# Two layers of graph convolution on one core: half of the attention transposes through VectorE's 32x32 blocks and DRAM

## What is computed

```python
h = max(layernorm(x), 0)                                  # 128 x 512
feats = einsum('nf,hfu->hnu', h, W)                       # 8 heads of 64 units
dense = leaky_relu(e_self[:, :, None] + e_neigh[:, None, :], 0.2)
att = softmax(dense + (-1e10) * (1 - A))                  # 8 x 128 x 128
x = x + relu(concat(att @ feats) + b)
h = max(layernorm(x), 0)
r = relu(hypergraph_conv(h, adj, W1, b1))                 # 128 x 1024
y = hypergraph_conv(layer_norm(r) * gamma + beta, adj, W2, b2)
out = x + (y + h)                                         # 128 x 512
```

## Time and profile before

| | before |
|---|---|
| median of three runs | 2489.99 us (2489.61 to 2491.07) |
| profiled execution, its own time | 2479.36 us |
| span of its instructions | 2477.6 us |
| TensorE (PE) busy | 2419.2 us, 98% |
| VectorE (DVE) busy | 1976.4 us, 80% |
| ScalarE (ACT) busy | 1763.3 us, 71% |
| GpSimd (POOL) busy | 1368.0 us, 55% |
| moved by DMA | 336.69 MB in 656793 packets |

### The profile page before, as it was taken

One profiled execution on the slowest core, in us unless ns is written; L12 is line 12 of the kernel. 1 busy time (PEld: TensorE's weight loads), 2 busy tenths in 40 slices (PEclk: granted clock), 3 DMA queues, 4 the chain that ended last, 5 costly groups with the idle time before them and its releaser, 6 DMA issues.

```text
span 2477.6 us, 50428 instructions
## 1 busy us (share of the span) xinstructions
PE 2419.2 (98%) x14004; PEld 2101.6 (85%) x14004; DVE 1976.4 (80%) x4373; ACT 1763.3 (71%) x4489; POOL 1368.0 (55%) x1549
## 2 busy tenths in 40 slices
PE   5799999999999999999999999999999999999997
PEld 3688888888888888888888888888888888888886
DVE  3888888888888888888888888888888888888884
ACT  2677777777777777777777777777777777777774
POOL 2465555565565565565555555555555556556543
PEclk8899999999999999999999999999999999999999
DMA  5344454455445445445445445445454444445442
GB/s 206 95 139 138 136 140 137 134 140 140 134 139 141 134 139 141 134 138 142 132 138 143 131 139 143 125 145 139 128 142 137 134 138 138 137 137 138 138 113 72
DMA packets 656793, 336.69 MB, mean 136 GB/s; under 512 B 554752, under 2 KB 571136, under 8 KB 656768
## 3 DMA queue, kind: packets, MB, share of 16 engines
q1 hardware_dynamic: 636256, 298.64, 43.5%
q10 hardware_dynamic: 20512, 37.76, 4.3%
HBM read 235.03 MB, written 101.26 MB: 136 GB/s over the span
## 4 chain that ended last, share of the span: by engine, by line
PE 95%; DMA 2%; DVE 1%; issue 1%; ACT 1%; POOL 0%; SPq 0%; POOLq 0%; DVEq 0%; ACTq 0%
PE p_w1a L853 15%; PE p_w1a L858 14%; PE p_w1a L854 14%; PE p_att L927 9%; PE p_w1b L854 5%; PE p_w1b L858 5%; PE p_w1b L853 5%; PE p_w1b L957 5%; PE p_att L907 4%; PE p_fa L849 3%; PE p_fa L847 3%; PE p_fa L848 3%; PE p_fb L847 2%; PE p_fb L848 2%; PE p_fb L849 2%; PE p_tb L847 1%
## 5 line engine op out<-in xcount | busy, mean ns | idle before, releaser
L338 POOL TENSOR_TENSOR u<-u,mask 128x1024 f32<-128x1024 f32 x128 | 306.6, 2395 | 761.4 <-DMA u<-en_rows 761.4
L438 ACT ACTIVATE att<-u,shifts 128x128 f32<-128x128 f32 x1024 | 402.3, 393 | 133.0 <-DVE shifts L740 131.6
L853 PE MATMUL p_w1a<-W_hi,rT_hi 128*128 128x512 f32 x1024 | 416.8, 407 | 1.5 <-ACT rT_hi L561 1.5
L854 PE MATMUL p_w1a<-W_lo,rT_hi 128*128 128x512 f32 x1024 | 405.9, 396 | 0.0
L439 ACT ACTIVATE att_low<-u,shifts 128x128 f32<-128x128 f32 x1024 | 399.6, 390 | 0.0
L731 DVE TENSOR_REDUCE neg_max<-u 128x8 f32<-128x1024 f32 x128 | 156.1, 1220 | 149.9 <-POOL u L338 149.9
L858 PE MATMUL p_w1a<-W_hi,rT_lo 128*128 128x512 f32 x1024 | 259.5, 395 | 0.0
L392 POOL TENSOR_TENSOR z_lo<-raw,z_hi 128x512 fp32r<-128x512 f32 x128 | 165.7, 1294 | 154.9 <-ACT z_hi L547 154.9
L927 PE MATMUL p_att<-feats,attT 128*128 128x65 f32 x2048 | 243.1, 272 | 3.1 <-ACT attT L483 3.1
L927 PEld LDWEIGHTS p_att<-feats,attT 128*128 128x128 f32 x2048 | 239.5, 192 | 3.9 <-ACT attT L483 3.9
L547 ACT ACTIVATE z_hi<-raw 128x512 fp32r<-128x512 f32 x128 | 81.1, 634 | 221.6 <-DVE raw L797 221.6
(11 more groups left out here) (121 smaller groups left out, 6759.7 us busy)
## 6 DMA issues: line engine op xcount, KB each, us to landing
u<-en_rows SPq DMA_DIRECT2D x130, 576.0 KB, 3.6
r_blocks<-raw SPq DMA_DIRECT2D x128, 512.0 KB, 2.6
raw<-r_blocks SPq DMA_DIRECT2D x512, 128.0 KB, 3.2
xT_in<-in_xT SPq DMA_DIRECT2D x128, 256.0 KB, 3.9
out<-raw SPq DMA_DIRECT2D x128, 256.0 KB, 2.0
x_in<-in_x ACTq DMA_DIRECT2D x124, 256.0 KB, 3.6
adj_in<-in_adj SPq DMA_DIRECT2D x128, 128.0 KB, 2.5
en_rows<-eT SPq DMA_DIRECT2D x520, 1.1 KB
```

The costliest lines, as they stand in the source:

```text
L338: nc.gpsimd.tensor_tensor(u[:, g.slot(2), 0:HEADS, :], u[:, g.slot(2), 0:HEADS, :], mask[:, :].unsqueeze(1).broadcast_to([P, HEADS, N]), A ...
L438: nc.scalar.activation(att[:, i, :], u[:, g.slot(2), i, :], ACT.Exp, bias=shifts[:, 0, i:i + 1])
L853: mm(dst, hi, w_hi, start=first, stop=False)
L854: mm(dst, hi, w_lo, start=False, stop=False)
```

## The change

Heads 4 to 7 stay as they were: transposed by TensorE (now four instructions) and copied out of PSUM by ScalarE (now 512 columns wide). Heads 0 to 3 take another way. VectorE transposes `att` of these heads by 32x32 blocks into a new tile attB, behind z in its turn, two graphs ahead (graph t+2 in turn t). One turn later SP writes attB to DRAM ahead of the attention terms, and reads it back behind the broadcast of u in four DMAs, one for each block column, in runs of 32 elements (128 bytes), straight into attT. TensorE now multiplies heads 4 to 7 first, then waits for the reads and multiplies heads 0 to 3.

Two more edits go with it. The attention terms (eT) are written to DRAM by one DMA of all 128 partitions instead of four of nine; en_rows has 32 rows for it. And the columns of W1 and of b1 are permuted on the host, so that the reads of r_blocks can take runs of 256 elements (1 KB) instead of 32; the copies to rT_hi and rT_lo then put the chunks in order through their access patterns (`rT_chunks`).

```diff
         neg_max = sb("neg_max", [P, HEADS])
+        attB = sb("attB", [P, HH * N])
         attT = sb("attT", [P, HEADS, N])
         rden = sb("rden", [P, HEADS])
...
         rT = raw[:, 0, DH:2 * DH]
+        rT_chunks = rT.rearrange("p (q k a) -> p k q a", q=4, a=32)
         rT_hi, rT_lo = sb("rT_hi", [P, DH], F32R), sb("rT_lo", [P, DH], F32R)
...
-        en_rows = nc.dram_tensor("en_rows", [ROWS, N], F32, kind="Internal").ap()
+        en_rows = nc.dram_tensor("en_rows", [32, N], F32, kind="Internal").ap()
...
+        att_blocks = nc.dram_tensor("att_blocks", [P, HH * N], F32, kind="Internal").ap()
...
+                if t.plus(1).within(NG):
+
+                    sp.wait_ge(s_attB, t.plus(1).count())
+                    sp.dma_start(att_blocks[:, :], attB[:, :]).then_inc(s_attB_out, 16)
                 if g.within(NG + 2):
 
                     sp.wait_ge(s_eT, g.count())
-                    for q in range(4):
-                        sp.dma_start(en_rows[:, 32 * q:32 * (q + 1)], eT[32 * q:32 * q + ROWS, :]).then_inc(s_en_out, 16)
-                    sp.wait_ge(s_en_out, g.count(per=64))
+                    sp.dma_start(en_rows.rearrange("h (q a) -> q h a", a=32), eT[:, :]).then_inc(s_en_out, 16)
+                    sp.wait_ge(s_en_out, g.count(per=16))
                     sp.dma_start(u[:, g.slot(2), :, :].rearrange("p h n -> p (h n)"),
-                                 en_rows.rearrange("(a h) n -> a (h n)", a=1).broadcast_to([P, ROWS * N])).then_inc(s_en_bc, 16)
+                                 en_rows[0:ROWS, :].rearrange("(a h) n -> a (h n)", a=1).broadcast_to([P, ROWS * N])).then_inc(s_en_bc, 16)
+                if t.plus(1).within(NG):
+
+                    sp.wait_ge(s_attB_out, t.plus(1).count(per=16))
+                    for c in range(4):
+                        sp.dma_start(attT[32 * c:32 * (c + 1), 0:HH, :].rearrange("b k (q a) -> b k q a", q=4),
+                                     att_blocks.rearrange("(q b) (k c a) -> c b k q a", q=4, c=4, a=32)[c]).then_inc(s_attD, 16)
                 g = t.plus(-2)
                 if g.within(NG):
 
@@ -289,8 +302,8 @@
                     sp.dma_start(r_blocks[:, :], rB).then_inc(s_rB_out, 16)
                     sp.wait_ge(s_rB_out, g.count(per=16))
                     for c in range(4):
-                        sp.dma_start(rT[32 * c:32 * (c + 1), :].rearrange("a (k q b) -> a k q b", q=4, b=32),
-                                     r_blocks.rearrange("(q a) (k c b) -> c a k q b", q=4, c=4, b=32)[c]).then_inc(s_rT, 16)
+                        sp.dma_start(rT[32 * c:32 * (c + 1), :].rearrange("a (q n) -> a q n", q=4),
+                                     r_blocks.rearrange("(q a) (c n) -> c a q n", q=4, c=4)[c]).then_inc(s_rT, 16)
...
                 act.wait_ge(s_shifts, g.count())
                 if g.has(1):
-                    act.wait_ge(s_attT, g.count(1))
+                    act.wait_ge((s_attB, s_attT)[half], g.count(1))
                     act.wait_ge(s_att, g.count(1, per=2))
...
-                    nc.scalar.activation(attT[:, :, :].rearrange("p h n -> p (h n)"), p_att[:, :],
+                    nc.scalar.activation(attT[:, HH:HEADS, :].rearrange("p h n -> p (h n)"), p_att[:, HALF:2 * HALF],
                                          ACT.Copy).then_inc(s_attT_sb, 1)
...
                     act.wait_ge(s_rT, g.count(per=64))
                     if g.has(1):
                         act.wait_ge(s_w2, g.count(1))
-                    nc.scalar.activation(rT_hi[:, :], rT, ACT.Copy).then_inc(s_rT_hi, 1)
+                    nc.scalar.activation(rT_hi[:, :].rearrange("p (k q a) -> p k q a", q=4, a=32), rT_chunks, ACT.Copy).then_inc(s_rT_hi, 1)
...
                     dve.wait_ge(s_rT_hi, g.count())
-                    nc.vector.tensor_tensor(rT_lo[:, :], rT, rT_hi[:, :], ALU.subtract).then_inc(s_rT_lo, 1)
+                    nc.vector.tensor_tensor(rT_lo[:, :].rearrange("p (k q a) -> p k q a", q=4, a=32), rT_chunks,
+                                            rT_hi[:, :].rearrange("p (k q a) -> p k q a", q=4, a=32), ALU.subtract).then_inc(s_rT_lo, 1)
...
                     nc.vector.scalar_tensor_tensor(z[:, :], p_w1a[:, :], rs2[:, g.slot(2):g.slot(2) + 1], t_bc[:, :],
                                                    ALU.mult, ALU.add).then_inc(s_z, 1)
+                g = t.plus(2)
+                if g.within(NG):
+
+                    dve.wait_ge(s_att, g.count(per=2) - 1)
+                    if g.has(1):
+                        dve.wait_ge(s_attB_out, g.count(1, per=16))
+                    nc.vector.transpose(attB[:, :], att[:, 0:HH, :].rearrange("p h n -> p (h n)")).then_inc(s_attB, 1)
...
                     pe.wait_ge(s_att, g.count(per=2))
                     if g.has(1):
                         pe.wait_ge(s_osc, g.count(1))
-                    for i in range(HEADS):
+                    for i in range(HH, HEADS):
                         last = nc.tensor.transpose(p_att[:, i * N:(i + 1) * N], att[:, i, :], ident[:, :])
                     last.then_inc(s_attT, 1)
...
                     pe.wait_ge(s_attT_sb, g.count())
                     pe.wait_ge(s_feats_sb, g.count(per=2))
-                    for i in range(HEADS):
-                        last = mm(p_o[:, i // HH, i % HH, :], attT[:, i, :], feats[:, g.slot(2), i, :], start=True, stop=True)
+                    for i in range(HH, HEADS):
+                        mm(p_o[:, i // HH, i % HH, :], attT[:, i, :], feats[:, g.slot(2), i, :], start=True, stop=True)
+                    pe.wait_ge(s_attD, g.count(per=64))
+                    for i in range(HH):
+                        last = mm(p_o[:, 0, i, :], attT[:, i, :], feats[:, g.slot(2), i, :], start=True, stop=True)
                     last.then_inc(s_o, 1)
...
+    def by_blocks(a):
+
+        return a.reshape(a.shape[:-1] + (-1, 4, 32)).swapaxes(-3, -2).reshape(a.shape)
...
-        "W1T": np.asarray(L1_gnn_W1).T, "b1": L1_gnn_b1,
+        "W1T": by_blocks(np.asarray(L1_gnn_W1).T), "b1": by_blocks(np.asarray(L1_gnn_b1)),
```

2 lines of the change are left out of this document (1 added, 1 removed).

## The result

The changed kernel takes 2475.11 us (median of four runs, 2472.43 to 2477.38) beside 2490.53 us for the kernel before in the same rounds (2489.61 to 2493.04). The ratio is 0.9938 with a 95% interval of 0.9924 to 0.9953: it is faster, by 0.6%. The forecast was 2439 us with a range up to 2466: the direction was right, but 15 of 51 us came.

The account below looks back on a forecast made before the run. TensorE was taken to bound the kernel: 55.4 us off for the transposes, less 2.5 for VectorE's lateness and 1.5 for the ramp, is 51.4, from 2489.99 to 2439 us. The range was 2430 to 2466.

Parts of the forecast that it names:

- Removed from TensorE: Four of eight transposes on TensorE go, 0.44 us per turn; over 126 turns 55.4 us off.
- Edge one: ScalarE's halved copy of transposed heads ends 0.13 us before TensorE's product wants it, as before.
- The block transpose: VectorE's new instruction with 512 elements per partition adds 0.65 us to the chain through u.
- The strided copies to rT_hi and rT_lo: Taking r's chunks in order by access pattern costs VectorE under 0.02 us each.
- From eT to eT: VectorE's chain from turn to turn through u takes 17.89 of 18.53 us, its waits for others being outside it.
- VectorE's idle time ahead of hg_lo shrinks: Sign expected in the profile after: this wait falls from 0.6 to under 0.2 us per turn.
- Edge two: Chain through u: transpose costs 0.65, single write gains 0.6; 17.94 us stays below TensorE's turn of 18.09.
- Edge three: Reads into attT, queued behind u, land 0.4 us before TensorE wants them; called the least certain edge.
- part of the gain is eaten by VectorE: Rival: smaller write gain or dearer VectorE work makes the chain through u bound the turn; 2448 to 2485 us, chance 0.23.

Follow-up runs that it names:

- e8: The kernel before, with ScalarE rounding hg_hi ahead of z_hi; ratio 0.995 to the kernel before.
- e7: The changed kernel with hg_hi rounded ahead of z_hi and VectorE's block transpose cut to 32 of 512 columns; ratio 0.9762 to the kernel before.
- e16: The changed kernel with hg_hi rounded ahead of z_hi and r's reads again in runs of 32 elements; ratio 0.9878 to the kernel before.
- The exchange: Two roundings on ScalarE swapped, hg_hi ahead of z_hi; in the changed kernel ratio 0.9875 to the kernel before, in the kernel before itself 0.995.
- e1: The changed kernel with the attention terms written by four DMAs of nine rows again; ratio 1.0073 to the kernel before.
- e17: The changed kernel with hg_hi rounded ahead of z_hi, without the write of attB and the reads into attT; ratio 0.9774 to the kernel before.
- e18: The changed kernel with hg_hi rounded ahead of z_hi, attB written but no reads into attT; ratio 0.9772 to the kernel before.
- e6: The changed kernel with ScalarE rounding hg_hi ahead of z_hi; ratio 0.9875 to the kernel before.
- e10: The changed kernel with hg_hi rounded ahead of z_hi and the first four heads' features computed behind eT; ratio 0.9869 to the kernel before.
- e15: The changed kernel with hg_hi rounded ahead of z_hi, two reads into attT ahead of u and two behind; ratio 1.0379 to the kernel before.
- e5: The changed kernel with the block transpose moved behind eT, rT_lo behind y and attB written behind the attention terms; ratio 1.0361 to the kernel before.
- e12: The changed kernel with hg_hi rounded ahead of z_hi and `larger` for half 0 ahead of the wait for G_rs; ratio 0.9898 to the kernel before.
- e9: The changed kernel: hg_hi ahead of z_hi, block transpose behind eT, attB written behind the terms, adj tests beside GpSimd's mask; ratio 1.0325 to the kernel before.

## Why the prediction was right in direction and wrong in size

- **Removed from TensorE, 0.44 us per turn**, was right. In the mean of the turns the transposes take 0.355 us from their first start to the next matmul instead of 0.792; the attention product in two parts takes 1.73 instead of 1.70. From e8 to e7, on the same chip, the turn went from 18.61 to 18.26 us, 0.35 us, and e7 still stands still for 0.09.
- **Edge one** held: the copy takes 0.58 us, and TensorE waits for ScalarE's part of attT 2.3 us in four times.
- **The block transpose** was priced at 0.65 us; it takes 0.63 in VectorE's queue. The strided copies to rT_hi and rT_lo cost nothing (1.05 and 1.21 us; with plain copies, e16, the time is the same).
- **The step that failed: "From eT to eT a turn has only these spots in which VectorE waits for something outside the chain: 0.42 us for hg_hi ... The chain itself thus takes 18.53 - 0.64 = 17.89 us."** hg_hi was not outside. It stood on ScalarE behind z_hi, which waited for VectorE's z. The chain was thus just below TensorE's turn and not 0.64 us below it: the row "changed" adds to 18.63 us where the prediction has 17.94. The transpose filled that wait and changed z to hg_lo from 2.03 to 2.05 us, so it cost next to nothing, but the room that was to take up every other lateness was not there. The exchange shows its share: 0.9938 to 0.9875, 16 us. The sign "VectorE's idle time ahead of hg_lo shrinks" came true and said nothing. (The 18.53 us are one turn; the mean is 18.65, which moves the chain and TensorE's turn alike.)
- **Edge two, the single write, gain 0.6 us**: the right mechanism, mis-sized. It measured 0.26 us, which e1 loses again. The issue itself takes 0.59 us, where I had allowed the 0.34 of a small DMA; the rest lies behind it: from the end of the issue to u's it is 1.41 us, 0.89 before. The spread over the engines was as assumed. The DMA queue in the half microsecond in which the terms move (packets, MB, share of 16 engines' time):

```profile
q1 hardware_dynamic: 129, 0.02, 20.5%
```

  That is 0.205 x 16 x 0.5 = 1.64 us of engine time, moved within some 0.4 us: about four engines. The rule of the Trainium skill that the prediction named (DMA: Bandwidth & Descriptors, "Why a DMA increments its semaphore by 16 and not by 1") gives four, and the trace agrees.
- **Edge three, the reads.** They are in time, as said. But I asked only whether u delays them, not whether they delay u. "Queue behind u on the same sixteen engines" made them harmless to u; they cost it 0.15 to 0.3 us per turn, on the chain: 1.0%, 26 us (with the exchange, e17 against e16). The prediction's sum has no term for this.
- Together: without reads and with the exchange the ratio is 0.977 (e17, e18). The forecast, 2439 / 2490, is 0.980. The two causes, 16 and 26 us, are together enough for the 36 us that were missing. How the 36 divide between them is not shown: each was measured on another base, and the exchange also gains 0.5% in the kernel before, which is no part of the forecast's error. With the exchange on both sides the change is worth 0.75% with the reads (e6, e8) and 1.8% without them (e17, e8), where 2.0% was forecast. The rival "part of the gain is eaten by VectorE" came nearest: its condition (the single write gains less) was met and 2475 us lies in its span of 2448 to 2485. Its price of 2457 us was missed, since it began from 17.89 too (and by its own terms is 2490 - 35 + 1.5 = 2456).

The best complete kernel is the changed one with hg_hi ahead of z_hi: 2455.11 us against 2487.22, ratio 0.9875 (e6); e10 is equal to it. A way to bring the blocks back without reads beside u was not found: in the turn they are needed 5.4 us after u's issue, and ahead of u they cost more (e15).

## What to carry to other kernels

A wait for another engine is room in the chain only if what the other engine did just before does not itself wait for this one: look up the releaser's predecessor in its own queue before counting idle time as slack. Where two strands are of like length, removing one shows nothing; an experiment has to shorten both. Read from the starts of the matmuls, not from the busy share, whether TensorE stands still: here 97% busy hid 0.38 us per turn. When a transfer is placed beside one that the chain waits for, price both ways, what it suffers and what it inflicts, and read a gap in a queue together with what runs beside it on the engines that share a resource.

## What the hardware showed that I had not expected

- VectorE and GpSimd hold each other up, by kind of instruction: GpSimd's mask took 3.12 instead of 2.37 us beside VectorE's TENSOR_TENSOR (e5), its root 0.90 instead of 0.55 (e12); VectorE's TENSOR_SCALAR of two columns took 0.81 instead of 0.17 us (e9). STREAM_TRANSPOSE beside the same mask kept 1.25 us. In the turn shown of e9 inc started while the mask ran and ended 0.17 us behind its end; in e5 rT_lo, which had started first, ended at 1208.62, 0.71 us behind the start of the mask, and the mask took 0.57 us longer. Whoever starts first is not slowed, the other waits. All turns of e5 bear this out: in 108 of 124 rT_lo started first and took 1.22 us, the mask 3.14 in the mean; in the other 16 the mask started first and took 2.38 us in the median, rT_lo 3.34. The Trainium skill says this (SBUF — State Buffer, "Who interferes with whom": an exclusive lock on the shared port pair, held for the instruction, between GpSimd and VectorE's operations with two SBUF inputs or in a 2-port mode); these runs agree, though no trace here names the mode of a TENSOR_SCALAR.
- A DMA of 128 short runs takes longer to issue than one of nine: 0.59 against 0.34 us. Three DMAs saved were worth 0.26 us, not 1.03.
- One read of 512 short runs next to u costs the kernel about 0.8%, four cost 1.0 to 1.5%: the first costs most. Why is open.
